# Three PSUM banks for both kinds of scores in a two-layer attention and expert kernel, half of layer 0's penalties laid by ScalarE

## What is computed

```python
x = x + tanh(g_xattn[0]) * attention0(layernorm(x), ctx, ctx, mask, W_q, W_k, W_v, W_proj, b_proj)
x = x + tanh(g_ffn[0])   * ffn0(layernorm(x), w_gate, w_up, w_down)      # quantized
x = x + tanh(g_xattn[1]) * attention1(layernorm(x), ctx, ctx, Wq, Wk, Wv, Wo, bo)
x = x + tanh(g_ffn[1])   * experts(layernorm(x), w_router, w_gate, w_up, w_down)   # 32 experts, top 1

# attention0, per batch and head (attention1 is the same without the mask)
scores = einsum('bhqd,bhkd->bhqk', Q, K) / sqrt(16)
scores = where(mask, scores, -1e10)
heads_out = einsum('bhqk,bhkd->bhqd', softmax(scores), V)
```

## Time and profile before

| what | value |
|---|---|
| median of 3 runs | 1262.97 us (1260.5 to 1263.43) |
| the profiled execution, its own time | 1267.7 us |
| its span | 1266.4 us |
| granted TensorE clock, mean | 0.983 |
| busy: PE, DVE, ACT, POOL | 94%, 70%, 56%, 38% |

### The profile page before, as it was taken

The page is one execution under the profiler, slowest core; times in us unless marked ns, Lnnn a source line. Parts: engine busy times, 40 slices in busy tenths (PEclk is TensorE's granted clock), DMA queues, the critical chain, the costliest instruction groups (busy, mean ns, idle before and its releaser), DMA issues.

```text
span 1266.4 us, 25147 instructions
## 1 busy us (share of the span) xinstructions
PE 1188.2 (94%) x9260; PEld 877.5 (69%) x9260; DVE 892.3 (70%) x2680; ACT 709.8 (56%) x1197; POOL 480.1 (38%) x677
## 2 busy tenths in 40 slices
PE   7799999999999989999999978999999999889998
PEld 6577777777777654444458866777777777578987
DVE  4687878877788446599999846768778778642343
ACT  2356556565656538899964425666666666622221
POOL 5445434443342000166001433443643643323555
PEclk9899999999999989999999999999999999988999
DMA  7424333433331050000004643364563442147973
GB/s 188 136 62 126 106 107 89 114 111 88 115 87 54 19 176 1 1 1 1 1 25 143 184 134 105 106 169 131 154 172 112 134 129 61 52 160 250 304 193 37
DMA packets 121941, 137.23 MB, mean 108 GB/s; under 512 B 12881, under 2 KB 116427, under 8 KB 121797
## 3 DMA queue, kind: packets, MB, share of 16 engines
q1 hardware_dynamic: 111888, 125.98, 33.5%
q0 software_dynamic: 7296, 8.15, 3.5%
q10 hardware_dynamic: 2634, 1.49, 0.5%
HBM read 58.42 MB, written 27.36 MB: 68 GB/s over the span
## 4 chain that ended last, share of the span: by engine, by line
PE 72%; DVE 9%; ACT 6%; issue 6%; POOL 3%; DMA 1%; ACTq 1%; SPq 1%; another core or an unknown queue 0%; POOLq 0%; DVEq 0%
PE PS L676 14%; PE PS L477 8%; PE PS L418 7%; PE PS L461 6%; PE PS L722 6%; PE PS L437 6%; PE PS L690 4%; PE PS L509 4%; PE PS L535 4%; PE PS L464 3%; PE PS L425 3%; ACT P L846 2%; PE PS L731 2%; DVE MX L1123 2%; DVE ON L1181 2%
## 5 line engine op out<-in xcount | busy, mean ns | idle before, releaser
L846 ACT ACTIVATE P<-PS 128x512 f32<-128x512 f32 x512 | 300.0, 602 | 125.0 <-PE PS L464 75.7
L461 PE MATMUL PS<-QS,KS 99*128 99x256 bf16 x1024 | 226.7, 274 | 14.4 <-ACT P L846 13.3
L1123 DVE CUSTOM_DVE_ANT_0 MX<-PS,NQ 128x256 bf16<-128x256 f32 x512 | 191.8, 417 | 56.1 <-PE PS L437 56.1
L1126 DVE TENSOR_REDUCE NM<-PS 128x2 f32<-128x512 f32 x256 | 172.2, 684 | 64.9 <-PE PS L437 64.5
L437 PE MATMUL PS<-KS,QS 96*128 96x256 bf16 x1024 | 195.4, 274 | 5.9 <-DMA QS<-PP 2.1
L461 PEld LDWEIGHTS PS<-QS,KS 99*128 99x128 bf16 x1024 | 92.7, 99 | 61.6 <-issue 23.3
L464 PE MATMUL PS<-NK,identb 128*128 128x256 bf16 x512 | 127.9, 274 | 0.0
L477 PE MATMUL PS<-P,V 128*32 128x256 f32 x2048 | 125.5, 386 | 1.2 <-ACT P L846 1.2
L676 PE MATMUL PS<-XNT,wup 128*128 128x512 f16 x576 | 124.9, 379 | 0.0
L437 PEld LDWEIGHTS PS<-KS,QS 96*128 96x128 bf16 x1024 | 96.6, 98 | 36.8 <-issue 10.2
L676 PEld LDWEIGHTS PS<-XNT,wup 128*128 128x128 f16 x576 | 56.2, 98 | 67.4
(11 more groups left out here) (234 smaller groups left out, 2465.1 us busy)
## 6 DMA issues: line engine op xcount, KB each, us to landing
KS<-PP SPq DMA_DIRECT2D x192, 128.0 KB, 3.1
QS<-PP SPq DMA_DIRECT2D x192, 128.0 KB, 2.7
WH<-in_wex SPq DMA_DIRECT2D x16, 768.0 KB
WG<-in_wex SPq DMA_DIRECT2D x10, 768.0 KB
bufd<-bias_row SPq DMA_DIRECT2D x5, 1032.0 KB, 12.4
XB<-in_x SPq DMA_DIRECT2D x16, 256.0 KB, 3.4
CT<-in_ctxT SPq DMA_DIRECT2D x16, 256.0 KB, 3.1
x1d<-XB SPq DMA_DIRECT2D x16, 256.0 KB, 2.1
```

The source lines that it names most:

```text
L461: ins = tensor.matmul(o, t.KS[b % 3][0:99, h, 128 * kt:128 * kt + 128], t.QS[b % 3][0:99, h, :], start=True, stop=(L == 1))
L846: scalar.activation(t.P[i % NP_RING][:, :, :], PS[:, h % 2, :].rearrange("p (k n) -> p k n", k=2), ACT.Exp).then_inc(s_ex, 1)
L1123: ins = vector.tensor_tensor_reduce(t.MX[:, 2 * score_turn(L, b, h) + qt, :], PS[:, bk, 256 * qt:256 * qt + 256], t.NQ[b % 4][:, qt, :], - ...
L1126: ins = vector.tensor_reduce(nm[:, :, h], PS[:, bk, :].rearrange("p (t n) -> p t n", t=2), X, ALU.max, negate=True)
```

## The change

The scores' banks become 2, 3 and 4; the transposed scores go round banks 0, 1 and 5 and wait for the exponential of three heads earlier. The values' products no longer have a bank: they take their turn in banks 6 and 7, and stand at the head of their slot on TensorE and on ScalarE (the copy `OT` moves from slots 10 and 2 to slots 9 and 1, ahead of the exponential). In layer 0 the two identity products of a head become one of 512 columns ahead of the scores, which add to it; for odd heads (but not head 1 of the first batch) there is none, and ScalarE writes the penalty into the bank instead (`act_penalty`), three heads ahead, in every other slot. Some semaphores are merged or dropped and the warm-up products go to another bank.

```diff
 def score_bank(L, b, h):
     if (L, b) == (1, 0) and h < 8:
         return 2 + h % 4
-    return (2, 3, 5)[score_turn(L, b, h)]
+    return 2 + turn_of(L, b, h)
...
+def laid_first(b, h):
+    return h % 2 == 1 and (b, h) != (0, 1)
+
+def score_t_bank(L, b, h):
+    return (0, 1, 5)[turn_of(L, b, h)]
...
         def pe_scores_t(L, b, h):
-            pe.wait_ge(s_ex, i - 1)
+            pe.wait_ge(s_ex, i - 2)
             if L == 0:
                 pe.wait_ge(s_pen, n + 1)
-            bk = h % 2
+            if L == 0 and laid_first(b, h):
+                pe.wait_ge(s_pre, i // 2)
+            bk = score_t_bank(L, b, h)
+            laid = L == 0 and laid_first(b, h)
+            if L == 0 and not laid:
+                tensor.matmul(PS[:, bk, :], identb[:, :], t.NK[b % 4][:, :, :].rearrange("p k n -> p (k n)"),
+                              start=True, stop=True)
             for kt in range(2):
-                o = PS[:, bk, 256 * kt:256 * kt + 256]
-                ins = tensor.matmul(o, t.KS[b % 3][0:99, h, 128 * kt:128 * kt + 128], t.QS[b % 3][0:99, h, :],
-                                    start=True, stop=(L == 1))
-                if L == 0:
-                    ins = tensor.matmul(o, identb[:, :], t.NK[b % 4][:, kt, :], start=False, stop=True)
+                ins = tensor.matmul(PS[:, bk, 256 * kt:256 * kt + 256], t.KS[b % 3][0:99, h, 128 * kt:128 * kt + 128],
+                                    t.QS[b % 3][0:99, h, :], start=(L == 1), stop=True, skip_group_check=(L == 0))
...
         def pe_av(L, b, hh):
+            bk = odd_bank(("av", n, hh), s_ot, 2 * n + hh + 1)
             pe.wait_ge(s_v, n + 1)
             pe.wait_ge(s_ex, 16 * n + 8 * hh + 8)
-            pe.wait_ge(s_ot, 2 * n + hh)
...
         def pe_slot(L, s, k):
+            if 0 <= s < NB and k == 9:
+                pe_av(L, s, 0)
+            if 0 <= s - 1 < NB and k == 1:
+                pe_av(L, s - 1, 1)
             if 0 <= s < NB:
                 pe_scores_t(L, s, k)
-                if k == 9:
-                    pe_av(L, s, 0)
...
+        def act_penalty(b, h):
+            i = 16 * b + h
+            act.wait_ge(s_pen, b + 1)
+            act.wait_ge(s_ex, i - 2)
+            scalar.activation(PS[:, score_t_bank(0, b, h), :].rearrange("p (k n) -> p k n", k=2), t0.NK[b % 4][:, :, :],
+                              ACT.Copy).then_inc(s_pre, 1)
...
         def act_slot(L, s, k):
+            if 0 <= s < NB and k == 9:
+                act_heads(L, s, 0)
+            if 0 <= s - 1 < NB and k == 1:
+                act_heads(L, s - 1, 1)
             if 0 <= s < NB:
                 act_exp(L, s, k)
+            ahead = 16 * s + k + 3
+            if L == 0 and 0 <= ahead < 16 * NB and laid_first(*divmod(ahead, 16)):
+                act_penalty(ahead // 16, ahead % 16)
             for b, hh in maxima_at(L, s, k, 10, 2):
                 act_maxima(L, b, hh)
-            if 0 <= s < NB and k == 10:
-                act_heads(L, s, 0)
```

More of the change, by code:

```diff
@@ L102, in scores_at, with turn_of @@
     return (k,)
-def score_turn(L, b, h):
+def turn_of(L, b, h):
     return (16 * (L * NB + b) + h) % 3
@@ L343, in build @@
         d_c = [sem(f"d_c{i}") for i in range(2)]
-        d_m = [sem(f"d_m{i}") for i in range(2)]
+        d_in = [sem(f"d_in{i}") for i in range(2)]
         d_w = {n: sem("d_w" + n) for n in "qkvo"}
@@ L355, in build @@
         s_evar, s_ers, s_xm, s_xmp, s_xmt = (sem(n) for n in ("s_evar", "s_ers", "s_xm", "s_xmp", "s_xmt"))
-        d_x1 = [sem(f"d_x1{i}") for i in range(4)]
+        d_out = [sem(f"d_out{i}") for i in range(4)]
         s_am = sem("s_am")
@@ L371, in build @@
         d_sc = [sem(f"d_sc{i}") for i in range(2)]
-        d_xe = [sem(f"d_xe{i}") for i in range(2)]
-        d_xf = [sem(f"d_xf{i}") for i in range(4)]
         s_et, s_xet, s_eg, s_si, s_eu, s_he, s_ey, s_ix, s_ye = (sem(n) for n in (
@@ L393, in rows_in @@
             if q == 0:
-                return (d_xf[0], 32) if i in (0, 4) else (d_xf[i], 16)
-            return d_xe[q % 2], 80 * (q // 2 + q % 2)
+                return (d_out[0], 96) if i in (0, 4) else (d_out[i], 80)
+            return d_in[q % 2], 16 * (NB // 2) + 80 * (q // 2 + q % 2)
         def odd_bank(job, emptier, value):
@@ L590, in pe_slot @@
                     if (L, b) == (0, 0):
-                        pe_warm(4, 12)
+                        pe_warm(5, 12)
                     pe_values(L, b)
             if 0 <= s - 1 < NB:
-                if k == 1:
-                    pe_av(L, s - 1, 1)
                 if k in (5, 6):
@@ L601, in pe_slot @@
                     if L == 1 and s == NB:
-                        pe_warm(4, 6)
+                        pe_warm(5, 6)
                     pe_out(L, s - 1)
@@ L606, in pe_slot @@
                     if s - 2 == NB - 1:
-                        pe_warm(4, 14)
+                        pe_warm(5, 14)
                     pe_xm(L, s - 2)
@@ L612, in pe_slot @@
                     if s - 2 == NB - 1:
-                        pe_warm(4, 10)
+                        pe_warm(5, 10)
                     pe_ranks(GROUP_OF[s - 2][0])
@@ L759, in pe_program @@
             pe.wait_ge(s_cst, 1)
-            pe_warm(4, 20)
+            pe_warm(5, 20)
             for s, k in slots(0):
                 pe_slot(0, s, k)
-            pe_warm(4, 6)
+            pe_warm(5, 6)
             pe.wait_ge(s_am, NB)
@@ L766, in pe_program @@
             pe_scale_b(0)
-            pe_warm(4, 13)
+            pe_warm(5, 13)
             for i in range(NCH):
@@ L803, in pe_program @@
             pe.wait_ge(s_pos, 6)
-            pe_warm(4, 30)
+            pe_warm(5, 30)
             pe_turn(0)
@@ L1136, in dve_any @@
             t = t0
-            dve.wait_ge(d_m[b % 2], 16 * uses(0, b, 2))
+            dve.wait_ge(d_in[b % 2], 16 * uses(0, b, 2))
             dve.wait_ge(s_rs, b - 1)
@@ L1448, in dve_ffn @@
             for i in range(4):
-                dve.wait_ge(d_x1[i], 64)
+                dve.wait_ge(d_out[i], 64)
             dve.wait_ge(s_am, NB)
@@ L1822, in sp_x1 @@
             sp.wait_ge(s_res, b + 1)
-            sync.dma_start(rows(x1d, b), t0.XB[b % 5][:, :, :]).then_inc(d_x1[b % 4], 16)
+            sync.dma_start(rows(x1d, b), t0.XB[b % 5][:, :, :]).then_inc(d_out[b % 4], 16)
         def sp_base(b):
@@ L1906, in sp_x1_load @@
         def sp_x1_load(b):
-            sp.wait_ge(d_x1[b % 4], 16 * uses(0, b, 4))
+            sp.wait_ge(d_out[b % 4], 16 * uses(0, b, 4))
             if b >= 3:
@@ L1939, in sp_program @@
                 sp_expert_rows(e)
-            sp.wait_ge(d_xf[0], 32)
+            sp.wait_ge(d_out[0], 96)
             for e in range(4, 8):
```

25 lines of the change are left out of this document (11 added, 14 removed).

## The result

The changed kernel takes 1244.33 us (median of 4 runs, 1242.64 to 1246.56), the kernel before 1262.92 beside it: a ratio of 0.986 [0.984, 0.988], 18.6 us less. The prediction was 1240, within 1226 to 1257, and faster. The two profiled executions lie further apart than the medians: 1267.7 and 1245.49, spans 1266.4 and 1244.2.

A forecast was written before the change was run, and what follows sets the result against it. TensorE, busy 94% of the span, was taken as the bound. Layer 0 keeping 12.6 of 29.7 us plus 10 us in layer 1 gave 22.6 off the profiled 1267.7, so a median of 1240 us, range 1226 to 1257.

The forecast's parts named there:

- What bounds the kernel: Whole kernel: TensorE is the bound, busy 94% of the span at a granted clock of 0.9 or more in every slice.
- TensorE's saving in layer 0: Layer 0's identity products: 57.6 us fall to 27.9, so TensorE saves 29.7 us, 1.87 per batch.
- First, the wait for `ON`: Layer 0, transposes of slot 8: they wait for VectorE's `ON`, so 3.6 us of the saving are lost over 15 batches.
- Third, ScalarE between the queries' projection and the values' products: Layer 0, slots 6 to 9: ScalarE's operations and two penalties nearly fill TensorE's 5.5 us; 0.3 lost per batch, 4.5 us.
- Second, VectorE: Layer 0: VectorE, 93% busy in weight-preparing batches, makes scores wait for maxima; 0.5 lost in every second batch, 4 us.
- Fourth, weights' batches: Layer 0's three batches with weight transposes: values' products wait for two ScalarE copies; 1.3 lost each, 4 us.
- Fifth, the last batch: Layer 0's last batch: without next batch's scores, ScalarE's 0.8 us per slot sets the pace in places; 1 us lost.
- The values' products in banks 6 and 7: Moving these products: costs nothing outside the three weight-transposing batches; if cover is gone, 0.6 us twice per batch.
- The third bank in layer 1: Layer 1: two waits for exponentials, 0.74 us per batch, become slack; 11 us over 15 batches, less 1, so 10.
- The sum: Whole kernel: 12.6 us kept in layer 0 plus 10 in layer 1 is 22.6 us, for a median of 1240.
- The rival in which ScalarE makes the kernel slower: Layer 0: penalties delay TensorE by more than 0.31 us each; at 0.4 each, 1274 us; chance 11%.
- The rival in which layer 0 gains nothing: Layer 0: losses at upper bounds, 14, 13 and 4 us, use up its gain; layer 1's 10 stays: 1253 us; 13%.

## Why the prediction came out right, and which terms were off

**What bounds the kernel: right, with one slip.** The granted clock was not 0.9 or more in every slice; four of the 40 digits of the earlier trace rows are an 8. The batches that the prices rest on are at 1.00, so nothing hangs on it.

**TensorE's saving in layer 0, 1.87 per batch.** Not measured by itself, but its prices hold. Replacing two products by one of 512 columns moved the period by 0.13 (0.136 by my prices), and each head laid among 1 to 3 by 0.21 to 0.22. The granted clock was full in the light batch, as I had it. The Trainium skill's page "TensorE: Matmul & The Clock Gate", section "Back-to-back issue gap", has 131 ns for sustained products of 512 columns; the trace does not agree, with 0.21 for the one at 200.30 and 0.2165 for 282 in a row.

**First, the wait for `ON`: wrong in form.** In the kernel before, VectorE's row did end last, as I had read, but by 0.1 only. It did not grow to 0.75 but stayed at 0.50, because two waits of ScalarE's making, `PP` and `XNT`, came ahead of it and used the time up.

**Third, ScalarE between the queries' projection and the values' products: the mechanism was wrong.** I had 5.5 us for TensorE there and took 0.54 off for the first and third terms together, 6.04; it is 6.02. Two errors cancel in it: heads 5 and 7 save 0.45 and not the 0.24 that I wrote, which makes 5.25, and the loss is 0.77. I also treated the two losses as a sum on TensorE. The runs show one stretch from the queries' product to the transposes of `ON` that other engines set: 5.15 without the penalties of heads 5 and 7, and 5.46 with them, since ScalarE's `PP` then holds up GpSimd and VectorE. Moving a wait within it changes nothing. A penalty also costs 0.7 and not 0.63.

**Second, VectorE: mis-sized.** I took 0.5 in every second batch; it is 0.43 in the light batch, which I had thought spared. I had reasoned from VectorE's share of busy time, and the kernel with less work on VectorE shows that in the light batch this is not what counts: the order behind the output projection is.

The three terms together explain the light batch: 1.87 - 0.77 - 0.43 = 0.67 against 0.73 measured. I had forecast 1.1. The runs give the same by heads, from the 24.42 of one product for every head: heads 1 and 3 take off 0.43, all that their products cost. Heads 9 to 15 take off 0.44 (23.99 to 23.55), half of 0.87, and the wait for maxima has the other half. Heads 5 and 7 add 0.32.

**Fourth, weights' batches: the mechanism right, each too dear.** I had 1.3 in each of three, 4 us. The run with the banks alone shows the wait that I described, 0.9 to 1.0 in each of four batches, and 4.3 us in all. With the 1.7 us of clock of the first taken off, some 2.6 are left by estimate, 0.6 or 0.7 each. After, these four batches took 26.94, 26.90, 26.34 and 25.96: they gained 0.7 together, where the products saved in them are 7.5.

**Fifth, the last batch: mis-sized, 1 us against 4.3.** ScalarE sets the pace there as I said, but the pace alone costs 2.5: the kernel with the lighter search takes 20.75 at full clock, where before has 18.20. Of that, 1.0 remains without any penalty of ScalarE in this batch (19.20). The other 1.8 of the 4.3 go with the clock, which fell in the profiled execution and in others did not. The trace of before has its own dip, to 0.53, later, at 444 to 450.

**The values' products in banks 6 and 7: nothing in a light batch, as costed.** The run with the banks alone has 24.55 against 24.60. The last batch I had not thought of; it takes 1.3 more, of which the batch ahead of it gives back 0.8.

**The third bank in layer 1: right, and a little small.** 22.82 became 22.08, my 0.74 exactly, and no transposed score product waits in that batch. The 10 us became 13.0. 4.3 of these are in the first batch: 2.8 of waits, which the earlier trace rows did not show, and by estimate 1.5 of a clock that was low there before. The others gave 8.7, less than 15 x 0.74, because in some of them maxima end last (23.80 to 23.62).

**The sum.** 22.6 forecast, 22.2 between the two profiled executions, 18.6 between the medians. Layer 0 gained 6.7 instead of 12.6, and 2.8 of the 6.7 came ahead of batch 2, in part because the granted clock of 20 to 60 us was 0.87 instead of 0.83. Layer 1 gave 3 us more than forecast, and 2.5 came outside the terms, 0.9 in the feed-forward net and 1.6 at the end. So the profiled pair met the sum partly by luck: losses of layer 0 were 23 us and not 17, 1.8 of them clock, and layer 1's surplus, half of it clock as well, made up for them in part. What was right was the order: TensorE is the bound, layer 0 loses most of what it saves, and it keeps enough that layer 1's bank is not the whole gain. The rival in which ScalarE makes the kernel slower needed 0.31 us lost for each penalty; in the light batch the penalties make one stretch 0.31 longer, 0.04 for each of eight. The rival in which layer 0 gains nothing is nearer: the kernel with the banks alone, at 1252.6, is it, and after is 8 us below.

One thing is left open: why the profiled pair lies 3.6 us further apart than the medians. The profiled execution of before, 1267.7, is 4.3 above the slowest of the runs beside it. Stretches of lower clock come and go and may be the reason: in another launch the kernel before took 1262.65 at a mean granted clock of 0.990 and 1270.70 at 0.982, and the profiled one has 0.983. But after's profiled execution has 0.982 and is only 1.2 above its median, so this is not shown.

## What to carry to other kernels

When TensorE is the bound on average, follow each chain that leaves it and comes back, and price what is saved inside such a chain at nothing: here 2 heads of 16 in it cost time, 3 outside it gave all they had in a light batch, and 4 ahead of another chain gave half. Read in the trace how long the stretch is (5.15 to 5.18 us in three traces) rather than how busy its engines are, and look for a second chain that is nearly level. Then look for an order that shortens it; here two operations of VectorE put earlier gave 14 us, where the whole change gave 18.6.

When a stage's last iteration has less to do on the bounding engine, plan it by itself: the same assignment of work that pays in the middle cost 1.2 to 1.6 us there at full clock.
